# Attention in a two-layer tower: score products for the next maxima moved between the score products, value products of four tiles in one row, squares last on VectorE

## The chip, the cores and the metric

The kernel runs on one core of one Trainium2 chip. The metric is the device time of one execution in microseconds (us), median over several executions. A core has five engines with a queue each, worked in order: TensorE (PE; its weight loads stand in the profile as PEld), VectorE (DVE), ScalarE (ACT), GpSimd (POOL) and SyncE (SP, used here for transfers). Engines wait for each other through semaphores only.

## What is computed

Thirty-two sequences of 512 tokens with 64 features go through an embedding and then four blocks, each added to its input: attention 0, a routed feed-forward block, attention 1, a mixture-of-experts block. Each block works on layer-normed features. The two attention blocks are what the change touches. Cut to the core:

```python
h = h + _L0_attn_ref(_layernorm(h), L0_attn_Wq, L0_attn_Wk)
# ... routed feed-forward ...
h = h + _L1_attn_ref(_layernorm(h), Wq, bq, Wk, bk, Wv, bv, Wo, bo)
# with, for q, k (and v) projected from the normed x:
scores = jnp.einsum('bsd,btd->bst', q, k) * d ** -0.5
weights = jax.nn.softmax(scores, axis=-1)
attn = jnp.einsum('bst,btd->bsd', weights, v)
```

## The kernel before, in words

All activations stay in on-chip memory (tensor `H`). The kernel goes through the phases one after the other: embedding, attention 0 (signals `a0`), routed block (`f0`), attention 1 (`a1`), mixture (`f1`). Each phase runs over the 32 sequences, one sequence per step, as a software pipeline: every engine has its own list of instructions for step i, and some of them work for sequences i+1 to i+5. The helpers `sweep` and `sweep4` run the step's body: a few steps written out at both ends and a hardware loop over the middle (steps 4 to 25, on PE and POOL 4 to 23). The order of the work is written by hand; there is no planner.

One step i of attention before the change, engine by engine:

- PE, `body` (L1033): `spread_max(i)` (L983, four small products that turn the negated row maxima of sequence i into a row; waits until all four maxima of i are there), `project(i+1)` (L965, L969 and L970), the turns of the normed features of i+2 (L927), the score products `scores(i, 0)` and `scores(i, 1)` (L997, two products each, L1005 and L1006; the first waits for ACT's copy of the maxima row, those from tile 2 on for the exponential of the tile two before), `turn_back(i-1)` (L941, L952, the output of the sequence before), `scores(i, 2)`, `scores(i, 3)`, `scores_for_max(i+1, 0)` and `(i+1, 1)` (L972, L980), `values(i, 0)` and `(i, 1)` (L1008, L1014), `scores_for_max(i+1, 2)` and `(i+1, 3)`, `values(i, 2)` and `(i, 3)`. `scores_for_max` writes its four tiles in turn to two banks, so that tiles 2 and 3 wait until the maxima of tiles 0 and 1 have been taken.
- DVE, `body` (L750): `squares_on` for i+4 (L646: square L648, sum L650, scale L652), `sum_on` for i+5 (L644), `low_parts(i+1)` (L726, L728; waits for ACT's `QH`), `finish(i-1)` (L737: reciprocal L741, product L743, addition to `H` L745; waits for PE's `turn_back`), `maxima(i+1)` (L731, four reductions L734, each waits for its `scores_for_max`).
- ACT, `body` (L500): output copy of i-1 (L486), the maxima row (L505), `QH` of i+1 (L492), four exponentials (L512), the copy of the turned features of i+2 (L464).
- POOL, `norms` (L407 on): for sequence i+4 the mean and the centring (L364, L370; these wait for DVE's sum), for i+3 the power (L376; waits for DVE's L652) and then three passes that make the normed features, L383 (waits until the value products that still read this buffer are done), L388 and L391.

The last step (i = 31) has no next sequence: no maxima, and the four value calls already stand behind each other. In it DVE also runs `meanwhile`: in attention 0 the first expert weights, in attention 1 `first_gate` (L863), whose masks PE turns with L1143 right behind the last `turn_back`.

Of the kernel before, what the change touches and what calls it, by code (L numbers as in the profile page):

```python
# [28 lines left out]
NT = SEQ // P  # L29
# [138 lines left out]
def known(i):  # L168
    return isinstance(i, int)


def has(i):

    return not known(i) or i < NSEQ


def tower_kernel(nc, tokens, route, pack, experts, out, ids_dram, pos_dram):
# [3 lines left out]
    with ExitStack() as ctx:  # L181
# [77 lines left out]
        def f32(ap):  # L259
            return ap.bitcast(F32)  # L260
# [319 lines left out]
        def _(dve):  # L580
# [62 lines left out]
            def norm_sum(s, i, par):  # L643
                v.tensor_reduce(stat[:, par, 0, :], hb(i), axis=AX, op=ALU.add).then_inc(s.sum_ready, 1)  # L644
# [65 lines left out]
            def sum_on(s, after, i, par):  # L710

                if has(i):
                    norm_sum(s, i, par)
                elif after is not None:
                    dve.wait_ge(s.h_done, i - NSEQ + 1)
                    norm_sum(after, i - NSEQ, par)

            def squares_on(s, after, i, par):
                if has(i):
                    norm_squares(s, i, par)  # L720
                elif after is not None:
                    norm_squares(after, i - NSEQ, par)

            def attention(s, after, base, meanwhile):

                def low_parts(i, par):  # L726
                    dve.wait_ge(s.qh_ready, i + 1)
                    v.tensor_tensor(Q2[:, par, :], bank[1][:, :], f32(QH[:, par, :]),  # L728
                                    ALU.subtract).then_inc(s.ql_ready, 1)

                def maxima(i, par):  # L731
                    for t in range(NT):
                        dve.wait_ge(s.s_ps, i * NT + (t + 1))
                        v.tensor_reduce(nmax[:, par, t:t + 1], bank[2 + t % 2][:, :], axis=AX, op=ALU.max,  # L734
                                        negate=True).then_inc(s.max_ready, 1)

                def finish(i, par):  # L737
                    o = bank[7][:, 0:NT * BACK].rearrange("p (t d) -> p t d", t=NT)
                    dve.wait_ge(s.back_ps, i + 1)
                    c = base + i * 2  # L740
                    v.reciprocal(rec[:, :], o[:, :, D]).then_inc(dve_chain, 1)  # L741
                    dve.wait_ge(dve_chain, c + 1)
                    v.tensor_tensor(ON[:, :, :], o[:, :, 0:D], over(rec[:, :], D), ALU.mult).then_inc(dve_chain, 1)  # L743
                    dve.wait_ge(dve_chain, c + 2)
                    v.tensor_tensor(hb(i), hb(i), ON[:, :, :], ALU.add).then_inc(s.h_done, 1)  # L745

                low_parts(0, 0)
                maxima(0, 0)

                def body(i, par):  # L750
                    squares_on(s, after, i + 4, par)
                    sum_on(s, after, i + 5, 1 - par)
                    if has(i + 1):
                        low_parts(i + 1, 1 - par)
                    if not known(i) or i >= 1:
                        finish(i - 1, 1 - par)
                    if has(i + 1):
                        maxima(i + 1, 1 - par)

                sweep(dve, body)  # L760
                meanwhile()
                finish(NSEQ - 1, 1)
# [124 lines left out]
        def _(pe):  # L887
# [74 lines left out]
            def attention(s, before, after, layer, meanwhile, rest_before=None):  # L962


                def project(i, par):  # L965
                    pe.wait_ge(s.x2_ready, i + 1)
                    if not known(i) or i >= 1:
                        pe.wait_ge(s.ql_ready, i)
                    mm(bank[1][:, :], AH[:, layer, :], X2[:, par, :], start=True, stop=False)  # L969
                    mm(bank[1][:, :], AL[:, layer, :], X2[:, par, :], start=False, stop=True).then_inc(s.q_ps, 1)  # L970

                def scores_for_max(i, par, t):  # L972

                    if t == 0:
                        pe.wait_ge(s.qh_ready, i + 1)
                    if t >= 2:
                        pe.wait_ge(s.max_ready, i * NT + (t - 1))
                    elif not known(i) or i >= 1:
                        pe.wait_ge(s.max_ready, i * NT + (t - 1))
                    mm(bank[2 + t % 2][:, :], QH[:, par, t * P:(t + 1) * P], X2[:, par, :],  # L980
                       start=True, stop=True).then_inc(s.s_ps, 1)

                def spread_max(i, par):  # L983

                    pe.wait_ge(s.max_ready, i * NT + NT)
                    if before is not None and known(i) and i == 0:
                        pe.wait_ge(before.h_done, NSEQ)
                    if not known(i) or i >= 1:
                        pe.wait_ge(s.m_ready, i)
                    if not known(i) or i >= 2:  # L990
                        pe.wait_ge(s.h_done, i - 1)
                    for t in range(NT):
                        last = mm(bank[7][:, t * P:(t + 1) * P], nmax[:, par, t:t + 1].to_broadcast([P, P]),  # L993
                                  IR[:, :], start=True, stop=True)
                    last.then_inc(s.m_ps, 1)

                def scores(i, par, kt):  # L997

                    if kt == 0:
                        pe.wait_ge(s.m_ready, i + 1)  # L1000
                    if kt >= 2 or not known(i) or i >= 1:
                        pe.wait_ge(s.e_ready, i * NT + (kt - 1))
                    cols = slice(kt * P, (kt + 1) * P)
                    o = bank[4 + kt % 2][:, :]
                    mm(o, X2[:, par, cols], QH[:, par, :], start=True, stop=False)  # L1005
                    mm(o, X2[:, par, cols], Q2[:, par, :], start=False, stop=True).then_inc(s.st_ps, 1)  # L1006

                def values(i, par, lane, kt):  # L1008

                    pe.wait_ge(s.e_ready, i * NT + (kt + 1))  # L1010
                    if kt == 0 and (not known(i) or i >= 1):
                        pe.wait_ge(s.ot_ready, i)
                    for h in range(2):
                        last = mm(bank[6][h * D:(h + 1) * D, 0:HALF], XN[:, lane, kt, :],  # L1014
                                  PT[:, par, kt, h * HALF:(h + 1) * HALF], start=(kt == 0), stop=(kt == NT - 1))
                    if kt == NT - 1:
                        last.then_inc(s.o_ps, 1)

                if before is None:
                    turn(s, 0, 0)  # L1020
                else:
                    pe.wait_ge(before.h0_ready, NSEQ)
                    pe.wait_ge(before.h1_ready, NSEQ)
                    pe.wait_ge(before.h2_ready, NSEQ)
                project(0, 0)
                if before is None:
                    turn(s, 1, 1)
                else:
                    rest_before()
                for t in range(NT):  # L1030
                    scores_for_max(0, 0, t)

                def body(i, par, lane):  # L1033
                    spread_max(i, par)
                    if has(i + 1):
                        project(i + 1, 1 - par)
                    turn_on(s, after, i + 2, par)
                    scores(i, par, 0)
                    scores(i, par, 1)
                    if not known(i) or i >= 1:  # L1040
                        turn_back(s, before, i - 1, 1 - par)
                    scores(i, par, 2)
                    scores(i, par, 3)
                    if has(i + 1):
                        scores_for_max(i + 1, 1 - par, 0)
                        scores_for_max(i + 1, 1 - par, 1)
                    if not has(i + 1):
                        pe.wait_ge(s.ql_ready, NSEQ)
                        meanwhile()
                    values(i, par, lane, 0)  # L1050
                    values(i, par, lane, 1)
                    if has(i + 1):
                        scores_for_max(i + 1, 1 - par, 2)
                        scores_for_max(i + 1, 1 - par, 3)
                    values(i, par, lane, 2)
                    values(i, par, lane, 3)

                sweep4(pe, body)
                turn_back(s, before, NSEQ - 1, 1)

# [247 lines left out]
```

## Time and profile before

| what | value |
|---|---|
| median of 3 runs | 1017.17 us (1013.14 to 1017.37) |
| the profiled execution's own time | 1015.07 us |
| its span, first to last instruction | 1013.3 us |
| mean granted TensorE clock | 0.978 of full speed |
| busy share of the span | PE 92%, PEld 62%, DVE 65%, ACT 53%, POOL 48% |
| attention 0 lies at about | 78 to 319 us |
| attention 1 lies at about | 461 to 705 us |

How to read it: the profile is one execution. Times in rows are microseconds from the span's start unless they are marked ns. A group's row gives the line of the kernel, the engine, the operation, output and input tiles and the count. A timeline row gives start, duration, engine, line and operation; "x8" merges neighbours of one kind, and the bracket is the idle time of the engine before it with what ended that. Matmuls are pipelined: the next one starts before the one before has ended.

### The profile page before, as it was taken

Reading aid. Unit: us, or ns where it says so; the run is one execution under the profiler, and the core shown is the slowest. Engines: PE = TensorE matmul, PEld = TensorE weight load, DVE = VectorE, ACT = ScalarE, POOL = GpSimd, SP = SyncE. Lnnn points to the kernel's source line nnn. Section 1 sums busy time; section 2 is a strip of 40 time slices with the busy share of each in tenths; the row PEclk is TensorE's granted clock in tenths of the full one; section 3 lists DMA queues with packets and bytes.
Section 4 is the critical chain, followed back from the end, with each engine's and each line's share of the span. In section 5 each row is a group of like instructions: output and inputs, shape, how many; then the busy total and the mean of one; then the engine's idle time right before and its main releaser. Section 6 shows DMA issues by size and latency. Waiting matters only on the chain.

```text
span 1013.3 us, 20527 instructions
## 1 busy us (share of the span) xinstructions
PE 927.8 (92%) x5964; PEld 631.8 (62%) x5964; DVE 661.0 (65%) x1864; ACT 540.6 (53%) x1065; POOL 490.1 (48%) x779
## 2 busy tenths in 40 slices
PE   0579999999998888888999999999999999999998
PEld 0456666666666555555666666666667666666665
DVE  1686787878887888886888888886343343343431
ACT  0234555555555555553555555556555665565564
POOL 0036555454546888894454545554434434434410
PEclk9867999999999999998999999999999999999999
DMA  8930000000000221210000000000000000000000
GB/s 8 278 99 1 2 0 0 0 0 0 1 1 29 56 63 56 59 53 1 1 1 0 0 0 0 1 1 1 12 12 16 16 10 16 16 10 16 16 11 22
DMA packets 31309, 22.35 MB, mean 22 GB/s; under 512 B 14498, under 2 KB 26914, under 8 KB 31266
## 3 DMA queue, kind: packets, MB, share of 16 engines
q1 hardware_dynamic: 31266, 21.81, 9.4%
q8 instruction: 23, 0.38, 0.2%
q14 instruction: 20, 0.16, 0.1%
HBM read 17.54 MB, written 4.26 MB: 22 GB/s over the span
## 4 chain that ended last, share of the span: by engine, by line
PE 72%; DVE 11%; POOL 7%; issue 5%; DMA 4%; DVEq 0%; ACT 0%; SPq 0%; POOLq 0%
PE bank L1179 11%; PE bank L1005 7%; PE bank L1014 7%; PE bank L1159 7%; PE bank L1006 6%; DVE nmax L734 6%; PE bank L1160 6%; PE bank L980 6%; PE bank L927 5%; PE bank L993 4%; PE bank L952 3%; POOL stat L376 2%; PE bank L1169 2%; PE bank L969 2%; DMA pos<-posn 2%
## 5 line engine op out<-in xcount | busy, mean ns | idle before, releaser
L383 POOL TENSOR_TENSOR XN<-XC,stat 128x252 f32<-128x252 f32 x128 | 85.4, 667 | 215.4 <-PE bank L1014 210.4
L734 DVE TENSOR_REDUCE nmax<-bank 128x1 fp32r<-128x512 f32 x256 | 165.0, 686 | 34.6 <-PE bank L980 30.1
L376 POOL TENSOR_TENSOR stat<-stat,half 128x4 f32<-128x4 f32 x128 | 134.3, 1049 | 91.2 <-DVE stat L652 88.6
L512 ACT ACTIVATE PT<-bank 128x512 f32<-128x512 f32 x256 | 139.4, 595 | 46.4 <-PE bank L1006 46.4
L1014 PE MATMUL bank<-PT,XN 128*64 128x256 f32 x1024 | 138.3, 392 | 0.0
L561 ACT ACTIVATE PT<-bank 128x512 f32<-128x512 f32 x256 | 132.0, 605 | 11.2 <-PE bank L1160 11.2
L486 ACT ACTIVATE OT<-bank 128x256 f32<-128x256 f32 x96 | 36.8, 383 | 183.4 <-PE bank L1014 132.0
L1179 PE MATMUL bank<-PT,W 128*64 128x256 f32 x1024 | 122.8, 382 | 0.0
L464 ACT ACTIVATE X<-bank 128x512 fp32r<-128x512 f32 x128 | 76.4, 597 | 80.1 <-PE bank L927 80.1
L1005 PE MATMUL bank<-QH,X 128*128 128x512 f32 x256 | 116.5, 455 | 0.4 <-ACT Q L505 0.4
L1159 PE MATMUL bank<-X,WH 128*128 128x512 f32 x256 | 108.0, 422 | 0.8 <-ACT K L552 0.8
L391 POOL TENSOR_TENSOR XS<-XN,XS 128x252 fp32r<-128x252 f32 x128 | 94.5, 738 | 18.7 <-POOL XS L388 0.5
L1006 PE MATMUL bank<-Q,X 128*128 128x512 f32 x256 | 102.1, 399 | 0.0
L927 PE MATMUL bank<-W,XS 128*128 128x128 f32 x512 | 82.0, 283 | 21.8 <-POOL XS L391 21.1
L1160 PE MATMUL bank<-K,WL 80*128 80x512 f32 x256 | 101.4, 396 | 0.0
L1014 PEld LDWEIGHTS bank<-PT,XN 128*64 128x64 f32 x1024 | 62.2, 136 | 58.1 <-ACT PT L512 22.8
L364 POOL TENSOR_TENSOR stat<-stat,ninv 128x4 f32<-128x4 f32 x128 | 30.7, 240 | 136.6 <-DVE stat L644 136.6
L927 PEld LDWEIGHTS bank<-W,XS 128*128 128x128 f32 x512 | 60.4, 143 | 54.2 <-POOL XS L391 24.1
L1179 PEld LDWEIGHTS bank<-PT,W 128*64 128x64 f32 x1024 | 70.4, 136 | 33.9 <-ACT PT L561 0.4
L980 PE MATMUL bank<-X,QH 128*128 128x512 f32 x256 | 88.3, 426 | 1.7 <-DVE nmax L734 1.4
L370 POOL TENSOR_TENSOR XC<-H,stat 128x256 f32<-128x256 f32 x128 | 79.1, 618 | 20.0 <-POOL stat L364 16.3
L826 DVE TENSOR_REDUCE g<-bank 128x32 f32<-128x64 f32 x32 | 7.2, 224 | 116.2 <-PE bank L1136 116.2
(124 smaller groups left out, 1656.6 us busy)
## 6 DMA issues: line engine op xcount, KB each, us to landing
WR<-experts SPq DMA_DIRECT2D x64, 129.0 KB, 2.1
PT<-ids SPq DMA_DIRECT2D x16, 256.0 KB, 5.3
out<-H SPq DMA_DIRECT2D x32, 128.0 KB, 1.7
posb<-pos SPq DMA_DIRECT2D x16, 192.0 KB, 5.7
W<-pack SPq DMA_DIRECT2D x5, 263.0 KB, 6.5
W<-pack SPq DMA_DIRECT2D x1, 262.5 KB, 8.6
W<-pack SPq DMA_DIRECT2D x1, 65.0 KB, 4.6
tk<-tokens SPq DMA_DIRECT2D x1, 64.0 KB, 4.4
```

What stands on the lines that cost most here:

```text
L376: pl.tensor_tensor(stat[:, par, 3, :], stat[:, par, 2, :], half[:, :], ALU.pow).then_inc(sigma_done, 1)
L512: sc_.activation(PT[:, par, kt, :], bank[4 + kt % 2][:, :], ACT.Exp, scale=SCALE).then_inc(s.e_ready, 1)
L561: sc_.activation(G[:, e, :], bank[UP[e % 4]][:, :], ACT.Gelu).then_inc(f1.gelu_ready, 1)
L734: v.tensor_reduce(nmax[:, par, t:t + 1], bank[2 + t % 2][:, :], axis=AX, op=ALU.max, negate=True).then_inc(s.max_ready, 1)
L927: last = nc.tensor.transpose(bank[0][:, t * P:(t + 1) * P], f32(XS[:, par, t, :]), w("ident"))
L980: mm(bank[2 + t % 2][:, :], QH[:, par, t * P:(t + 1) * P], X2[:, par, :], start=True, stop=True).then_inc(s.s_ps, 1)
L1005: mm(o, X2[:, par, cols], QH[:, par, :], start=True, stop=False)
L1006: mm(o, X2[:, par, cols], Q2[:, par, :], start=False, stop=True).then_inc(s.st_ps, 1)
L1014: last = mm(bank[6][h * D:(h + 1) * D, 0:HALF], XN[:, lane, kt, :], PT[:, par, kt, h * HALF:(h + 1) * HALF], start=(kt == 0), stop=(kt == ...
L1159: mm(o, WH[:, a:a + HID], X2[:, par, :], start=True, stop=False)
L1160: mm(o, WL[0:D + 2 * NEXP1, a:a + HID], K2[0:D + 2 * NEXP1, par, :], start=False, stop=True)\
L1179: last = mm(bank[5 + par][h * D:(h + 1) * D, 0:HALF], w2[:, e, :], G[:, e, h * HALF:(h + 1) * HALF], start=False, stop=(e == NEXP1 - 1))
```

## The change

On PE the four `scores_for_max` of the next sequence move: tile 0 goes between `scores(i, 1)` and `turn_back`, tile 1 between `scores(i, 2)` and `scores(i, 3)`, tiles 2 and 3 behind `scores(i, 3)`. The four `values` calls then follow each other without anything between. On DVE the four maxima are parted: two behind `low_parts`, then `finish`, then two more; squares and sums go to the end of the step. No instruction is added or removed, and buffers and semaphores stay as they are.

```diff
@@ -728,8 +728,8 @@
-                def maxima(i, par):
-                    for t in range(NT):
+                def maxima(i, par, tiles):
+                    for t in tiles:
                         dve.wait_ge(s.s_ps, i * NT + (t + 1))
                         v.tensor_reduce(nmax[:, par, t:t + 1], bank[2 + t % 2][:, :], axis=AX, op=ALU.max,
                                         negate=True).then_inc(s.max_ready, 1)
@@ -745,17 +745,18 @@
                 low_parts(0, 0)
-                maxima(0, 0)
+                maxima(0, 0, range(NT))
 
                 def body(i, par):
-                    squares_on(s, after, i + 4, par)
-                    sum_on(s, after, i + 5, 1 - par)
                     if has(i + 1):
                         low_parts(i + 1, 1 - par)
+                        maxima(i + 1, 1 - par, range(2))
                     if not known(i) or i >= 1:
                         finish(i - 1, 1 - par)
                     if has(i + 1):
-                        maxima(i + 1, 1 - par)
+                        maxima(i + 1, 1 - par, range(2, NT))
+                    squares_on(s, after, i + 4, par)
+                    sum_on(s, after, i + 5, 1 - par)
@@ -1037,23 +1038,22 @@
                     turn_on(s, after, i + 2, par)
                     scores(i, par, 0)
                     scores(i, par, 1)
+                    if has(i + 1):
+                        scores_for_max(i + 1, 1 - par, 0)
                     if not known(i) or i >= 1:
                         turn_back(s, before, i - 1, 1 - par)
                     scores(i, par, 2)
+                    if has(i + 1):
+                        scores_for_max(i + 1, 1 - par, 1)
                     scores(i, par, 3)
                     if has(i + 1):
-                        scores_for_max(i + 1, 1 - par, 0)
-                        scores_for_max(i + 1, 1 - par, 1)
+                        scores_for_max(i + 1, 1 - par, 2)
+                        scores_for_max(i + 1, 1 - par, 3)
                     if not has(i + 1):
                         pe.wait_ge(s.ql_ready, NSEQ)
                         meanwhile()
-                    values(i, par, lane, 0)
-                    values(i, par, lane, 1)
-                    if has(i + 1):
-                        scores_for_max(i + 1, 1 - par, 2)
-                        scores_for_max(i + 1, 1 - par, 3)
-                    values(i, par, lane, 2)
-                    values(i, par, lane, 3)
+                    for kt in range(NT):
+                        values(i, par, lane, kt)
```

## Rows read from the trace of the kernel before

**Rows 1.** The page, busy time by engine over the whole span.

```profile
PE 927.8 (92%) x5964; PEld 631.8 (62%) x5964; DVE 661.0 (65%) x1864; ACT 540.6 (53%) x1065; POOL 490.1 (48%) x779
```

**Rows 2.** Line L505, one per step: attention 0, attention 1, loop of attention 0.

```profile
L505 ACT ACTIVATE Q<-bank x31: 586/587/589, 92.3 to 312.0; 1x512 fp32r<-1x512 f32 x31
...
L505 ACT ACTIVATE Q<-bank x30: 586/587/591, 477.6 to 690.0; 1x512 fp32r<-1x512 f32 x30
...
L505 ACT ACTIVATE Q<-bank x20: 586/587/589, 121.6 to 261.1; 1x512 fp32r<-1x512 f32 x20
```

**Rows 3.** Chain that ended last, end of one step: start, duration, what.

```profile
274.23 0.69 DVE nmax L734
```

**Rows 4.** Timeline of PE over one step of attention 0: start, duration, instruction.

```profile
267.70 0.66 PE L993 MATMUL bank<-IR,nmax 128*128 128x128 f32 x4
...
269.85 0.40 PE L1006 MATMUL bank<-Q,X 128*128 128x512 f32 x1
270.08 0.61 PE L952 MATMUL bank<-W,OT 128*128 128x130 f32 x4
...
270.80 0.40 PE L1006 MATMUL bank<-Q,X 128*128 128x512 f32 x1
...
271.52 0.62 PE L980 MATMUL bank<-X,QH 128*128 128x512 f32 x2
272.07 1.08 PE L1014 MATMUL bank<-PT,XN 128*64 128x256 f32 x8
273.08 0.72 PE L980 MATMUL bank<-X,QH 128*128 128x512 f32 x2
...
274.96 0.33 PE L993 MATMUL bank<-IR,nmax 128*128 128x128 f32 x1
```

**Rows 5.** Timeline of DVE over the same step.

```profile
269.54 0.69 DVE L728 TENSOR_TENSOR Q<-bank,QH 128x512 fp32r<-128x512 f32 x1 [0.19 <-ACT QH L492]
270.73 0.18 DVE L741 RECIPROCAL rec<-bank 128x4 f32<-128x4 f32 x1 [0.49 <-PE bank L952]
...
271.51 0.42 DVE L745 TENSOR_TENSOR H<-H,ON 128x256 f32 x1
...
273.62 1.29 DVE L734 TENSOR_REDUCE nmax<-bank 128x1 fp32r<-128x512 f32 x2 [0.38 <-PE bank L980]
274.82 0.41 DVE L648 TENSOR_TENSOR SQ<-XC 128x256 f32<-128x256 f32 x1
```

**Rows 6.** Timeline of ACT over the same step: the first two exponentials.

```profile
269.81 1.09 ACT L512 ACTIVATE PT<-bank 128x512 f32<-128x512 f32 x2 [0.30 <-PE bank L1006]
```

**Rows 7.** Timeline from L648 to POOL's L364 where nothing else stands between.

```profile
467.28 0.42 DVE L648 TENSOR_TENSOR SQ<-XC 128x256 f32<-128x256 f32 x1
...
468.26 0.41 DVE L644 TENSOR_REDUCE stat<-H 128x4 f32<-128x256 f32 x1
...
468.76 0.20 POOL L364 TENSOR_TENSOR stat<-stat,ninv 128x4 f32<-128x4 f32 x1 [5.84 <-DVE stat L644]
```

**Rows 8.** Timeline of POOL before the first step, where it waits for nothing.

```profile
80.77 0.20 POOL L364 TENSOR_TENSOR stat<-stat,ninv 128x4 f32<-128x4 f32 x1
...
84.03 0.72 POOL L391 TENSOR_TENSOR XS<-XN,XS 128x252 fp32r<-128x252 f32 x1
```

**Rows 9.** Timeline around the end of attention 0: L745 beside L391.

```profile
319.09 0.73 POOL L391 TENSOR_TENSOR XS<-XN,XS 128x252 fp32r<-128x252 f32 x1
...
319.53 0.57 DVE L745 TENSOR_TENSOR H<-H,ON 128x256 f32<-128x256 f32 x1
```

**Rows 10.** Timeline of POOL in the step of rows 4: the power.

```profile
270.69 1.02 POOL L376 TENSOR_TENSOR stat<-stat,half 128x4 f32<-128x4 f32 x1
```

**Rows 11.** Timeline of the last step of attention 1: values in one row, masks.

```profile
700.87 1.95 PE L1014 MATMUL bank<-PT,XN 128*64 128x256 f32 x16
...
702.59 0.17 DVE L852 TENSOR_SCALAR MK<-took 128x32 bf16<-128x32 f32 x1
...
703.85 0.39 PE L1143 MATMUL bank<-IB,MK 128*128 128x128 bf16 x4
```

## The prediction

> **What bounds the kernel now.** I read the page first: PE is busy 92% of the span, no other engine over 65% [rows 1]. A busy PE is not a PE without gaps, so I went to the attention phases, the only ones touched. One ACT instruction per step marks the period: attention 0 has 30 periods from 92.3 to 312.0, 7.32 us each; attention 1 has 29 from 477.6 to 690.0, also 7.32; the loop steps of attention 0 take 139.5/19 = 7.34 [rows 2]. So 62 periods (31 in each phase) of about 7.32 us, some 454 us, are what the change can touch.
>
> Next, one step by engine. It starts with the spread of the maxima at 267.70 and the next one starts at 274.96: 7.26 us, a step outside the loop [rows 4]. The chain that ended last goes through PE for most of the step, but its last piece is the fourth maximum on DVE, 274.23 to 274.91, and the spread follows 0.05 later [rows 3, 4]. PE had no work for the last stretch: the value row of eight that starts at 272.07 lets the next product start 1.01 later (273.08), 0.07 before its busy time is over; the second row ends in the same way at about 274.75, so PE waits some 0.2 us for DVE. A second cost is inside PE: each change between the value products and the 512-column products is dear. From 272.07 the value row, two score products and the second value row need 2.7 us, while sixteen value rows in one go are busy 1.95 [rows 4, 11].
>
> **The change part by part.** Times below count from the spread of a step (267.70 = 0).
>
> *PE.* The products up to `scores(i, 1)` stay: its last starts at 2.15, the next instruction at 2.38 [rows 4]. Tile 0 for the maxima now takes that place, and like two in a pair (0.62 busy, 0.23 apart) its result is there 0.39 later, at 2.77. `turn_back` starts at 2.61; from its start to the last product of `scores(i, 2)` are 0.72 us (270.08 to 270.80), so 3.33. Tile 1 starts at 3.56, result 3.95. `scores(i, 3)` and the step to the next product took 0.72 (270.80 to 271.52, of which 0.23 are that last product's own), so tile 2 starts at 3.56 + 0.72 = 4.28 and tile 3 could start at 4.51. Sixteen value products follow 0.32 after tile 3 (271.52 + 0.23 to 272.07) and hold PE for 1.95 - 0.07 = 1.88. Without a wait PE would need 6.71 us a step. The exponentials do not get in the way: the first two start at 2.11, end by 3.20, and the score products that wait for them now start at 2.99 and 3.79 [rows 6].
>
> *DVE.* `low_parts` starts at 1.84, when ACT's `QH` is there, and ends at 2.53 [rows 5]. Maximum 0 starts 0.04 after its product, at 2.81; maximum 1 after its own, at 3.99, for 0.69. A DVE instruction with nothing to wait for starts 0.08 before the last one ends (274.82 against 273.62 + 1.29). So `finish` starts at 4.60 and lasts 1.20, from 270.73 to the end of the addition at 271.93 [rows 5]: 5.80. Maxima 2 and 3 as a pair take 1.29 from 5.72: 7.01, and the next spread starts at 7.06.
>
> *The new wait.* Tile 3 needs maximum 1 out of its bank, which ends at 4.68: PE's in-order queue stands from 4.51 to 4.73. Behind it are the sixteen value products, so they start at 5.05 to 5.15 (the higher end if the weight load, hidden before, is now exposed for 0.1) and PE is free at 6.93 to 7.03. That is a hair before DVE. Both come out near the same time; DVE's 7.06 sets the period.
>
> *Squares and sums* move from ahead of `low_parts` to the end of the step, which is the same place in time: behind the last maximum, beside the next spread. On a free DVE they reach POOL's mean 1.48 us after they start [rows 7], so at 1.35 of the next step, before `low_parts` at 1.84. They are covered by that wait for `QH`; if it were gone they would cost up to 1.4 us. But they work for one sequence later than before. POOL's train from mean to the end of L391 takes 80.77 to 84.75, 3.98 us, if nothing holds it [rows 8], so it ends at 5.33. The PE turn that needs it comes at 1.0 of the step after, 8.1 on this count: 2.7 us of slack. No SP queue or DMA of this phase is moved.
>
> *Ends of phases.* In attention 1's last step squares and sum (1.39, [rows 7]) come between `finish` and `first_gate`. The masks were ready at 702.76 and used at 703.85 [rows 11]: 0.3 us late now. In attention 0 I find cover for the same shift (POOL waits for the last values there) and cost it nothing; without that cover it would be the 1.39 us at most.
>
> *Sum.* Loop steps take 0.08 longer than 7.26 today, and I keep half of it: 7.10 instead of 7.34, 0.24 x 40 = 9.6. Outside the loop 0.20 x 22 = 4.4. Less 0.3: 13.7 us. Against the profiled execution's own 1015.07 us (span 1013.3 and 1.8 around it) that is 1001.4. The median of the runs shown, 1017.17, is 2.1 higher, so about 1003. The unseen costs have two ends. If no DVE instruction starts early behind another engine's signal, two overlaps of 0.08 go: period 7.22, gain 6 us, 1011. If DVE proves shorter, PE's 6.93 decides: 24 us, 993. I take the early start, since it stands in the same timeline, behind the same kind of wait.
>
> **POOL beside `finish`: a row against a rule.** The addition to `H` reads two tensors of on-chip memory. Beside POOL's L391 it took 0.57 instead of 0.42: it ended at 320.10, 0.28 after POOL at 319.82 [rows 9]. Beside POOL's power, 270.69 to 271.71, it kept its 0.42 from 271.51 [rows 5, 10]. So the three passes block it, the power does not. In the new order the train's last pass ends at 5.33 and the addition starts at 5.38: just clear, and harmless up to 5.52, because 5.52 + 0.28 = 5.80 is when it ends anyway.
>
> The Trainium skill, "SBUF — State Buffer", section "SBUF: two separate sides", says that VectorE and GpSimd share one port pair as an exclusive lock: a VectorE operation with two SBUF inputs and a GpSimd operation block each other for the whole instruction. The trace agrees for L391 and differs for the power, where the rule would have the addition start at 271.71. By the rule the sum here stays as it is as long as the passes end before the addition; it speaks against the change otherwise, which is the second rival.
>
> **The rivals.**
>
> 1. *No change to speak of.* DVE's line from tile 1 to the spread is now maximum, `finish`, two maxima without a gap, 3.1 us, where before only a pair of maxima (1.3) hung on the last products. If register work for the loop's waits and the lost overlaps add 0.15 to 0.25 a step, the period is 7.21 to 7.31 and the time 1010 to 1016. For it: in the loop a step costs 0.08 more already. Against it: the same waits with their register work all stand in the loop today, and together they cost no more than that 0.08. Chance 0.17.
>
> 2. *Slower: POOL's passes hold up `finish`.* If POOL's train runs 0.4 us later than counted (its passes are slowed, or sum and mean come late), L391 lies across the addition. It decides from a train's end at 5.33 + 0.45 = 5.78 on, where the addition ends 0.26 late and the gain is gone. The worst is an addition that meets the whole of the pass: 0.73 + 0.28 instead of 0.42, 0.59 late, period 7.65, 62 x 0.33 = 20 us slower, 1037; halfway some 1024. For it: the margin is 0.05 us. Against it: a pass that late needs a delay for which no row speaks, since squares, sum and train are counted from stretches in which DVE and POOL were working as they will here [rows 7, 8]. Chance 0.11.
>
> 3. *More than forecast.* The maxima get ahead and PE alone decides, at 6.9: 1017 - 62 x 0.4 = 992 to 997. It needs DVE's line to lose 0.15 us, for which I see no source. Chance 0.10.
>
> **How the numbers follow.** The forecast has 0.62, with 999 to 1009 as its own range; the rivals 0.17, 0.11 and 0.10. The range leaves out the slower rival and about half of the third, and cuts the second half of the first: 996 to 1013. A measurement of this kernel can tell about 0.5%, 5 us, from no change, which is 0.08 us a period. Faster by more than that: the forecast, the third rival: 0.72. Within: 0.17. Slower: 0.11.
>
> **What would show it.** Right: L505 periods of 7.05 to 7.15; sixteen value products in one row of 1.95; a wait of PE for the maximum ahead of tile 3 of about 0.2; the last maximum still ending 0.05 before the spread; L391 ending before L745, and L745 at 0.42; `low_parts` still waiting for `QH`. Wrong: L745 over 0.6, `low_parts` starting after 1.9 because squares and sum ran into it, turns of PE waiting for POOL, or periods that stay at 7.3.

## The result, and the profile after

The median goes from 1016.5 us (1013.14 to 1017.37, 4 runs) to 1002.18 us (1001.87 to 1003.85, 4 runs): ratio 0.9866, 95% interval 0.9846 to 0.9887. That is 14.3 us, or 1.3%, faster; 1003 us was forecast. The profiled execution took 1001.87 us (span 1000.0). TensorE's granted clock was 1.00, the 2.4 GHz level, over nearly all of both attention phases (95 to 310 and 480 to 695 us in the kernel before, 95 to 303 and 475 to 681 in the changed one), so the gain there is not one of the clock.

The page, busy time by engine, against [rows 1]:

```profile
PE 914.0 (91%) x5964; PEld 640.0 (64%) x5964; DVE 635.4 (64%) x1864; ACT 547.3 (55%) x1065; POOL 485.6 (49%) x779
```

The same instructions, with 14 us less of busy PE time. A matmul's end is modelled and neighbours overlap, so this figure says little: by the page the group of value products is busy 13.7 us less (138.3 before, 124.6 now), the group of products for the maxima 21.1 more (88.3 and 109.4). The periods tell the gain. Line L505, all 32 of each attention (in the second fence the kernel before):

```profile
L505 ACT ACTIVATE Q<-bank x32: 586/587/590, 85.5 to 305.3; 1x512 fp32r<-1x512 f32 x32
L505 ACT ACTIVATE Q<-bank x32: 586/587/588, 462.9 to 683.2; 1x512 fp32r<-1x512 f32 x32
```

```profile
L505 ACT ACTIVATE Q<-bank x32: 586/587/589, 83.4 to 312.0; 1x512 fp32r<-1x512 f32 x32
L505 ACT ACTIVATE Q<-bank x32: 586/587/591, 468.6 to 697.3; 1x512 fp32r<-1x512 f32 x32
```

From these four rows the whole difference of the two spans can be laid out. Attention 0 takes 219.8 instead of 228.6 (-8.8), attention 1 takes 220.3 instead of 228.7 (-8.4): 0.277 us a period over 62. Between the two lie 157.6 instead of 156.6 (+1.0), behind the second 316.8 instead of 316.0 (+0.8), and ahead of the first 85.5 instead of 83.4 (+2.1). The sum is -13.3, the difference of the spans. The last item I put down to chance: the change moves nothing ahead of attention 0, and in the seven experiments below that stretch ended between 84.5 and 87.9. There is only one trace of the kernel before, so this is not shown.

One step of attention 0 outside the loop, PE, against [rows 4] (lines from about L750 to L1050 are one higher in the changed kernel):

```profile
262.56 0.66 PE L994 MATMUL bank<-IR,nmax 128*128 128x128 f32 x4
...
264.94 0.39 PE L981 MATMUL bank<-X,QH 128*128 128x512 f32 x1
265.16 0.61 PE L953 MATMUL bank<-W,OT 128*128 128x130 f32 x4
...
266.08 0.39 PE L981 MATMUL bank<-X,QH 128*128 128x512 f32 x1
...
266.76 0.99 PE L981 MATMUL bank<-X,QH 128*128 128x512 f32 x2
267.68 1.95 PE L1015 MATMUL bank<-PT,XN 128*64 128x256 f32 x16
269.57 0.33 PE L994 MATMUL bank<-IR,nmax 128*128 128x128 f32 x1
```

7.01 us from spread to spread. Tiles 0 and 1 stand at 2.38 and 3.52 of the step. The pair of tiles 2 and 3 is busy 0.99 instead of the 0.62 of an undisturbed pair [rows 4]: that is the wait for maximum 1 and the weight load behind it (last section). The value row starts at 5.12 and lasts 1.95. DVE and POOL over the same step, against [rows 5, 8]:

```profile
264.40 0.69 DVE L728 TENSOR_TENSOR Q<-bank,QH 128x512 fp32r<-128x512 f32 x1 [0.54 <-ACT QH L492]
265.36 0.69 DVE L734 TENSOR_REDUCE nmax<-bank 128x1 fp32r<-128x512 f32 x1 [0.27 <-PE bank L981]
266.50 0.69 DVE L734 TENSOR_REDUCE nmax<-bank 128x1 fp32r<-128x512 f32 x1 [0.45 <-PE bank L981]
267.11 0.17 DVE L741 RECIPROCAL rec<-bank 128x4 f32<-128x4 f32 x1
267.32 0.42 DVE L743 TENSOR_TENSOR ON<-bank,rec 128x256 f32<-128x256 f32 x1
267.89 0.43 DVE L745 TENSOR_TENSOR H<-H,ON 128x256 f32 x1
268.24 1.28 DVE L734 TENSOR_REDUCE nmax<-bank 128x1 fp32r<-128x512 f32 x2
269.43 0.41 DVE L648 TENSOR_TENSOR SQ<-XC 128x256 f32<-128x256 f32 x1
```

```profile
263.95 0.20 POOL L364 TENSOR_TENSOR stat<-stat,ninv 128x4 f32<-128x4 f32 x1 [3.02 <-DVE stat L644]
...
267.21 0.72 POOL L391 TENSOR_TENSOR XS<-XN,XS 128x252 fp32r<-128x252 f32 x1
```

From the second maximum on (266.50) DVE has no idle bracket: the gaps between its instructions are 0.15 us at most, and an instruction that does not need the result of the one above it starts 0.08 to 0.09 before that one ends. The last maximum ends at 269.52, the spread follows at 269.57. POOL's L391 ends at 267.93 and the addition starts at 267.89: they touch, without effect here.

### The profile page after: what moved, and what is told of

Its sections match the earlier page's. It is cut to its first block, busy times and chain, and to the rows that moved or that the text cites. A ratio compares the mean times of both kernels' runs of the same rounds, so it can differ in the third digit from the quotient of the medians.

```text
span 1000.0 us, 20527 instructions
## 1 busy us (share of the span) xinstructions
PE 914.0 (91%) x5964; PEld 640.0 (64%) x5964; DVE 635.4 (64%) x1864; ACT 547.3 (55%) x1065; POOL 485.6 (49%) x779
## 4 chain that ended last, share of the span: by engine, by line
PE 67%; POOL 12%; DVE 9%; issue 7%; DMA 5%; SPq 0%; POOLq 0%; ACT 0%; DVEq 0%
PE bank L1179 12%; PE bank L1015 9%; PE bank L1159 7%; PE bank L1160 6%; PE bank L981 5%; PE bank L928 5%; DVE nmax L734 4%; PE bank L1006 4%; POOL stat L376 4%; PE bank L1007 4%; PE bank L994 3%; PE bank L953 2%; POOL XN L383 2%; POOL XS L388 2%; DMA pos<-posn 2%
## 5 line engine op out<-in xcount | busy, mean ns | idle before, releaser
L734 DVE TENSOR_REDUCE nmax<-bank 128x1 fp32r<-128x512 f32 x256 | 170.1, 685 | 48.6 <-PE bank L981 48.4
L364 POOL TENSOR_TENSOR stat<-stat,ninv 128x4 f32<-128x4 f32 x128 | 30.6, 239 | 332.3 <-DVE stat L644 332.3
L512 ACT ACTIVATE PT<-bank 128x512 f32<-128x512 f32 x256 | 146.0, 596 | 61.6 <-PE bank L1007 56.5
L376 POOL TENSOR_TENSOR stat<-stat,half 128x4 f32<-128x4 f32 x128 | 134.4, 1050 | 91.1 <-DVE stat L652 88.6
L561 ACT ACTIVATE PT<-bank 128x512 f32<-128x512 f32 x256 | 132.0, 605 | 11.2 <-PE bank L1160 11.2
L1015 PE MATMUL bank<-PT,XN 128*64 128x256 f32 x1024 | 124.6, 385 | 0.0
L981 PE MATMUL bank<-X,QH 128*128 128x512 f32 x256 | 109.4, 430 | 7.6 <-DVE nmax L734 1.1
L1006 PE MATMUL bank<-QH,X 128*128 128x512 f32 x256 | 113.1, 442 | 0.4 <-ACT Q L505 0.4
L391 POOL TENSOR_TENSOR XS<-XN,XS 128x252 fp32r<-128x252 f32 x128 | 94.2, 736 | 18.7 <-POOL XS L388 0.5
L1015 PEld LDWEIGHTS bank<-PT,XN 128*64 128x64 f32 x1024 | 67.8, 136 | 43.3 <-ACT PT L512 15.3
L383 POOL TENSOR_TENSOR XN<-XC,stat 128x252 f32<-128x252 f32 x128 | 77.7, 607 | 10.8 <-POOL stat L376 1.6
```

Of the source, the lines that this page charges most:

```text
L376: pl.tensor_tensor(stat[:, par, 3, :], stat[:, par, 2, :], half[:, :], ALU.pow).then_inc(sigma_done, 1)
L512: sc_.activation(PT[:, par, kt, :], bank[4 + kt % 2][:, :], ACT.Exp, scale=SCALE).then_inc(s.e_ready, 1)
L561: sc_.activation(G[:, e, :], bank[UP[e % 4]][:, :], ACT.Gelu).then_inc(f1.gelu_ready, 1)
```

## The experiments

All were timed in three rounds against the kernel before on the same chip.

**1. Squares last, alone.** On the kernel before:

```diff
 def body(i, par):
-    squares_on(s, after, i + 4, par)
-    sum_on(s, after, i + 5, 1 - par)
...
     maxima(i + 1, 1 - par)
+    squares_on(s, after, i + 4, par)
+    sum_on(s, after, i + 5, 1 - par)
```

> The kernel before with one part of the change: squares and sums at the end of the DVE step, PE order untouched. My theory: the squares stay in the same place in time, so they give nothing; POOL's train from mean to L391 (3.98 us from 1.35 of the step) now lies across finish, whose addition should start at 3.81 and can be held until 0.28 after a pass of POOL, so the period goes from 7.35 to 7.35-7.55 and the time to 1016-1030 us (ends of the phases +1.8). Rival 'the squares are what gained' (the scale L652 drops from 0.57 to 0.17 and POOL's passes leave the spread): most of the 14 us, 1003-1007 us.

Measured: 1018.78 against 1017.1 us, ratio 1.0033 (1.0015 to 1.0050). The rival falls: the moved squares give nothing. Attention 0 takes 228.2 (85.3 to 313.5) and attention 1 228.7 (471.2 to 699.9), as before. The small loss lies at the ends of the phases: 157.7 us between the two instead of 156.6, and 316.8 behind the second instead of 316.0. In the steps POOL's passes did fall on `finish`. One step outside the loop of experiment 1, then all additions in the loop of attention 0:

```profile
272.54 0.61 POOL L383 TENSOR_TENSOR XN<-XC,stat 128x252 f32<-128x252 f32 x1
273.01 0.42 DVE L745 TENSOR_TENSOR H<-H,ON 128x256 f32 x1
273.11 0.80 POOL L388 TENSOR_TENSOR XS<-XC,stat 128x252 fp32r<-128x252 f32 x1
...
275.13 1.29 DVE L734 TENSOR_REDUCE nmax<-bank 128x1 fp32r<-128x512 f32 x2 [0.39 <-PE bank L980]
```

```profile
L745 DVE TENSOR_TENSOR H<-H,ON x19: 445/511/594, 118.8 to 251.1; 128x256 f32 x19
```

In the step shown the addition met only the last 0.14 of POOL's L383 and kept its 0.42; the next pass, L388, came behind the addition and took 0.80 where it takes 0.60 alone. In the loop every addition was held: 0.51 is the median and 0.59 the longest. The period did not grow for it, because DVE behind it still waits 0.39 for PE's next product for a maximum. So `finish` had slack here, which it loses in the new order.

**2. The row, alone.** On the kernel before, DVE as it was:

```diff
                         scores_for_max(i + 1, 1 - par, 1)
+                        scores_for_max(i + 1, 1 - par, 2)
+                        scores_for_max(i + 1, 1 - par, 3)
...
-                    values(i, par, lane, 0)
-                    values(i, par, lane, 1)
-                    if has(i + 1):
-                        scores_for_max(i + 1, 1 - par, 2)
-                        scores_for_max(i + 1, 1 - par, 3)
-                    values(i, par, lane, 2)
-                    values(i, par, lane, 3)
+                    for kt in range(NT):
+                        values(i, par, lane, kt)
```

> The kernel before with one part of the change: all four products for the next maxima ahead of the values, the sixteen value products in one row, DVE as before. My theory: tiles 2 and 3 then wait for maxima 0 and 1 (ends at 4.95 and 5.54 of a step) with nothing in between; tile 3 starts at 5.6, values at 5.93 and take 1.88: period 7.8, +0.45 to +0.5 a step over 62 steps, 1044-1048 us. Rival 'the row alone gains, through fewer changes between the two kinds of product': 0.25-0.33 a step less, 996-1002 us.

Measured: 1055.34 against 1017.1 us, ratio 1.0383 (1.0357 to 1.0409), slower by 38 us, some 8 more than expected. PE in experiment 2:

```profile
272.94 1.10 PE L980 MATMUL bank<-X,QH 128*128 128x512 f32 x2 [0.55 <-DVE nmax L734]
273.97 1.95 PE L1014 MATMUL bank<-PT,XN 128*64 128x256 f32 x16
275.84 0.66 PE L993 MATMUL bank<-IR,nmax 128*128 128x128 f32 x4
```

Tiles 2 and 3 each wait for a maximum, 0.55 us for the first and inside the 1.10 for the second; the row stands behind them. The row by itself is no gain: in the kernel before, the first two value calls were the work that covered those waits. Experiment 4 shows the other half.

**3. Squares first again.** On the changed kernel, `squares_on` and `sum_on` back to the head of the DVE step.

```diff
 def body(i, par):
+    squares_on(s, after, i + 4, par)
+    sum_on(s, after, i + 5, 1 - par)
...
     maxima(i + 1, 1 - par, range(2, NT))
-    squares_on(s, after, i + 4, par)
-    sum_on(s, after, i + 5, 1 - par)
```

> The changed kernel with squares and sums put back to the head of the DVE step. My theory: the period stays at 7.00-7.10 and low_parts still waits for QH; the ends of the two phases get back 1.0 + 0.8 us: 999-1002 us, the same or 1-2 us faster than the change. Rival 'squares last is a needed part': the period goes back to 7.2-7.3, 1010-1016 us.

Measured: 998.77 against 1017.1 us, ratio 0.9814 (0.9789 to 0.9840). That is 0.5% better than the change (0.9866, 0.9846 to 0.9887), and the two intervals just miss each other. The traces show about half of it. The attention phases last about what they last in the change, 219.6 and 219.4. What differs most is their ends. The end of attention 1 in the changed kernel, then in experiment 3:

```profile
686.23 0.42 DVE L745 TENSOR_TENSOR H<-H,ON 128x256 f32<-128x256 f32 x1
686.29 0.83 POOL L388 TENSOR_TENSOR XS<-XC,stat 128x252 fp32r<-128x252 f32 x1
686.57 0.83 DVE L648 TENSOR_TENSOR SQ<-XC 128x256 f32<-128x256 f32 x1
...
690.23 0.17 DVE L853 TENSOR_SCALAR MK<-took 128x32 bf16<-128x32 f32 x1
690.55 0.38 PE L1143 MATMUL bank<-IB,MK 128*128 128x128 bf16 x4 [0.61 <-DVE MK L853]
```

```profile
689.20 0.17 DVE L853 TENSOR_SCALAR MK<-took 128x32 bf16<-128x32 f32 x1
689.91 0.71 PE L953 MATMUL bank<-R,OT 128*128 128x130 f32 x4 [0.48 <-ACT OT L486]
690.46 0.39 PE L1143 MATMUL bank<-IB,MK 128*128 128x128 bf16 x4
```

With the squares last PE waits 0.61 for the masks; with the squares first they are ready before the last `turn_back`. So the third part of the change was a small loss, at the end of each phase: 156.9 us between the two attentions here (307.5 to 464.5), 157.6 in the change, 156.6 before; behind the second 316.0 here and before, 316.8 in the change. Experiment 1 has the same two losses by itself.

**4. Two value rows.** On the changed kernel, tiles 2 and 3 for the maxima back between the value calls; tiles 0 and 1 stay early.

```diff
-                        scores_for_max(i + 1, 1 - par, 2)
-                        scores_for_max(i + 1, 1 - par, 3)
...
-                    for kt in range(NT):
-                        values(i, par, lane, kt)
+                    values(i, par, lane, 0)
+                    values(i, par, lane, 1)
+                    if has(i + 1):
+                        scores_for_max(i + 1, 1 - par, 2)
+                        scores_for_max(i + 1, 1 - par, 3)
+                    values(i, par, lane, 2)
+                    values(i, par, lane, 3)
```

> The changed kernel with tiles 2 and 3 for the maxima put back between the two pairs of value products; tiles 0 and 1 stay early, DVE as in the change. My theory: tile 2's result comes at 5.80 of a step instead of 4.6, maxima 2 and 3 end at 7.13, period 7.18-7.25, 1010-1014 us: the row is worth about 10 us because it lets the last maxima start early. Rival 'early tiles alone carry it': 1002-1004 us as with the change.

Measured: 1011.41 against 1017.1 us, ratio 0.9943 (0.9926 to 0.9959). DVE in experiment 4:

```profile
277.74 0.43 DVE L745 TENSOR_TENSOR H<-H,ON 128x256 f32<-128x256 f32 x1
278.37 1.29 DVE L734 TENSOR_REDUCE nmax<-bank 128x1 fp32r<-128x512 f32 x2 [0.19 <-PE bank L981]
```

The addition ends at 278.17, and DVE then waits 0.19 for tile 2's product, which comes behind eight value products. By the ratios, early tiles 0 and 1 give some 6 us (0.9943), with DVE in the new order and its loss at the ends of the phases included, and the row on top of them some 8 (0.9866). The parted maxima on DVE were not tried by themselves.

**5. Tile 1 directly behind tile 0.** On the changed kernel:

```diff
                         scores_for_max(i + 1, 1 - par, 0)
+                        scores_for_max(i + 1, 1 - par, 1)
                     if not known(i) or i >= 1:
                         turn_back(s, before, i - 1, 1 - par)
                     scores(i, par, 2)
-                    if has(i + 1):
-                        scores_for_max(i + 1, 1 - par, 1)
```

> The changed kernel with one product moved: tile 1 for the maxima directly behind tile 0, ahead of turn_back. It takes PE's wait for maximum 1 away (end 4.1 of a step instead of 4.63, tile 3 wanted at 4.43). If nothing else held, PE alone would need 6.64 us a step. My theory: finish then starts at 4.02 and its addition at 4.80, under POOL's L391 (4.65 to 5.37), so that it ends 0.28 behind it, at 5.65 instead of 5.23; the last maximum ends at 6.85, period 6.90 (loop 6.95), 992-996 us. Rival 'POOL's passes do not hold DVE': 6.65-6.72, 977-982 us.

Measured: 990.2 against 1016.76 us, ratio 0.9728 (0.9696 to 0.9759), a little under the expected 992 to 996. POOL, DVE and PE in experiment 5:

```profile
276.70 0.72 POOL L391 TENSOR_TENSOR XS<-XN,XS 128x252 fp32r<-128x252 f32 x1
```

```profile
276.78 0.93 DVE L745 TENSOR_TENSOR H<-H,ON 128x256 f32<-128x256 f32 x1
277.63 1.27 DVE L734 TENSOR_REDUCE nmax<-bank 128x1 fp32r<-128x512 f32 x2
```

```profile
272.10 0.66 PE L994 MATMUL bank<-IR,nmax 128*128 128x128 f32 x4 [0.24 <-DVE nmax L734]
...
276.29 0.61 PE L981 MATMUL bank<-X,QH 128*128 128x512 f32 x2
```

The pair of tiles 2 and 3 is busy 0.61: no wait for a maximum is left in it. The price is where it was expected: the addition starts 0.08 after POOL's L391 and ends at 277.71, 0.29 after POOL's end at 277.42. The maxima behind it are late, and PE waits 0.24 for them. Not every step pays this in full: in the loop of attention 0 the additions take between 0.43 and 0.98, with a median of 0.87.

**6. `finish` cut short.** On the changed kernel:

```diff
-v.tensor_tensor(ON[:, :, :], o[:, :, 0:D], over(rec[:, :], D), ALU.mult).then_inc(dve_chain, 1)
+v.tensor_tensor(ON[:, :, 0:1], o[:, :, 0:1], over(rec[:, :], 1), ALU.mult).then_inc(dve_chain, 1)
...
-v.tensor_tensor(hb(i), hb(i), ON[:, :, :], ALU.add).then_inc(s.h_done, 1)
+v.tensor_tensor(hb(i)[:, :, 0:1], hb(i)[:, :, 0:1], ON[:, :, 0:1], ALU.add).then_inc(s.h_done, 1)
```

> The changed kernel with finish cut short: the product and the addition to H work on one of 64 columns only (the other 63 columns of both attention outputs are left out), some 0.5 us off DVE's line from maximum 1 to the last maximum. My theory: in the changed kernel two lines end a step at the same time, DVE's and PE's row of values, which starts late because tile 3 waits for maximum 1; cutting DVE's leaves PE's at 6.98-7.00, so 999-1002 us. Rival 'DVE's line alone sets the period': 6.64 a step, 977-980 us.

Measured: 997.93 against 1016.76 us, ratio 0.9804 (0.9772 to 0.9835). DVE and PE in experiment 6:

```profile
274.03 1.28 DVE L734 TENSOR_REDUCE nmax<-bank 128x1 fp32r<-128x512 f32 x2
```

```profile
273.19 0.99 PE L981 MATMUL bank<-X,QH 128*128 128x512 f32 x2
274.11 1.95 PE L1015 MATMUL bank<-PT,XN 128*64 128x256 f32 x16
275.99 0.66 PE L994 MATMUL bank<-IR,nmax 128*128 128x128 f32 x4
```

The last maximum is there at 275.31, 0.68 before the spread, and nothing comes of it: the pair still takes 0.99 and the row behind it ends the step. Attention 0 takes 218.5 (86.2 to 304.7) instead of 219.8, attention 1 218.8 (461.8 to 680.6) instead of 220.3. The first period of a phase differs from trace to trace (7.0 to 9.5 us over all nine); without it the phases are 1.1 and 0.9 shorter. So in the changed kernel two lines end a step within a few hundredths of each other, and shortening DVE's alone is worth about 1 us a phase. Another 0.5 and 0.7 us are saved behind the phases (157.1 and 316.1 instead of 157.6 and 316.8), where `finish` is shorter as well. The rest of the distance between the medians is not laid out.

**7. Both.** The edits of experiments 3 and 5 together.

> Both edits on the changed kernel: tile 1 directly behind tile 0, and squares and sums at the head of the DVE step, so that POOL's three passes run at the step's start again, away from finish. My theory: no wait of PE for a maximum is left and the addition keeps its 0.42; PE alone sets the step at 6.64-6.70, 976-980 us. Rival 'another wait takes its place' (low_parts, exponentials): 6.85 or more, 990 us and up.

Measured: 974.99 against 1016.76 us, ratio 0.9586 (0.9555 to 0.9616), a little under the expected 976 to 980. PE and DVE in experiment 7:

```profile
271.46 0.66 PE L994 MATMUL bank<-IR,nmax 128*128 128x128 f32 x4
...
276.20 1.95 PE L1015 MATMUL bank<-PT,XN 128*64 128x256 f32 x16
278.08 0.66 PE L994 MATMUL bank<-IR,nmax 128*128 128x128 f32 x4
```

```profile
276.13 0.43 DVE L745 TENSOR_TENSOR H<-H,ON 128x256 f32<-128x256 f32 x1
276.48 1.28 DVE L734 TENSOR_REDUCE nmax<-bank 128x1 fp32r<-128x512 f32 x2
```

The step is 6.62 us. The addition has its 0.43 back, the last maximum ends at 277.76, 0.32 before the spread, and the spread follows the value row at once. PE is the bound. This version beats both kernels: by 4.1% the one before, and by 2.8% the change (0.9586 against 0.9866).

## Why the prediction was right, point by point

*The period.* 7.06 was forecast outside the loop, 7.10 in it; measured are 7.01 in the step shown and, in the loop, 127.1/18 = 7.06, so 0.04 to 0.05 less than forecast:

```profile
L505 ACT ACTIVATE Q<-bank x19: 586/587/589, 122.1 to 249.2; 1x512 fp32r<-1x512 f32 x19
```

The steps of the working stand in the timeline: tile 0 at 2.38 (2.38), tile 1 at 3.52 (3.56), maximum 1 at 3.94 (3.99), values at 5.12 (5.05 to 5.15), last maximum's end at 6.96 (7.01). The 0.05 stand ahead of maximum 1; from there to the end of the last maximum it is 3.02, as forecast. The early start of DVE instructions is there too: the reciprocal at 267.11, 0.08 before maximum 1 ends. The end without it (1011) is out. One sign of the forecast did not come: L391 was to end 0.05 before the addition starts, and it ended 0.04 after, which costs nothing in the step shown.

*The wait for maximum 1.* PE's line behind it was forecast to end a hair before DVE's, and experiment 6 shows that the two are even. Experiments 5 and 7 show what it is worth once the other line is short as well.

*The row.* The prediction put its gain down to fewer changes on PE. Experiments 2 and 4 show that this gain can be had only with the early tiles: with late maxima the row costs 38 us, with early ones it brings 8. How much of the 8 is fewer changes and how much the earlier start of the last maxima, which wait for tile 2 in experiment 4, no run separates.

*Squares and sums.* In the steps their move gains nothing, as said: experiments 1 and 3. `low_parts` waits 0.54 for `QH`, so they stay covered.

*Ends of phases.* This term was mis-sized: 0.3 and 0 were forecast, 0.8 and 1.0 measured. In attention 1 I had costed the squares from a stretch without POOL [rows 7]. The last step has no maxima, so the squares come right behind `finish`: POOL's L388 had to wait for the addition L745 and took 0.83 instead of 0.60, and the square L648 had to wait for L388 and took 0.83 instead of 0.42 (rows under experiment 3). PE waited 0.6 for the masks instead of 0.3. In attention 0 the shift is not the 1.39 that the prediction called the most. The squares and the sum of the last step now stand behind its `finish`, which waits for `turn_back`. POOL there, in the kernel before and in the changed one:

```profile
317.78 0.61 POOL L383 TENSOR_TENSOR XN<-XC,stat 128x252 f32<-128x252 f32 x1 [2.48 <-PE bank L1014]
```

```profile
310.47 0.32 POOL L364 TENSOR_TENSOR stat<-stat,ninv 128x4 f32<-128x4 f32 x1 [0.47 <-DVE stat L644]
```

The mean L364 starts 5.2 us after the last L505 in the changed kernel (310.47) and 1.4 after it in the kernel before (313.43): a shift of 3.7. The cover was POOL's wait of 2.48 for the last values, and it is used up: L383 starts 7.3 after the last L505 instead of 5.8.

Two misses hide each other in the total: the periods gave 17.2 us instead of 14.0, the ends took 1.8 instead of 0.3, and the profiled execution's start was 2.1 later, which I put down to chance.

*The slower rival.* Its mechanism is real, and no more than a small part of it came: it decides from 5.78 for the end of POOL's train, which ended at 5.37. In the loop it already shows. L745 in the loop of attention 0, changed kernel:

```profile
L745 DVE TENSOR_TENSOR H<-H,ON x20: 424/427/520, 119.7 to 253.9; 128x256 f32 x20
```

Half stay at 0.43 or below, the longest is 0.52, so 0.09 late. In experiment 3, with POOL's passes elsewhere, none is over 0.43, and without their first periods the two phases take 0.8 and 0.3 us less. In experiment 5 the addition came 0.65 earlier in the step (4.68 instead of 5.33) and ran fully into L391: 0.93. The Trainium skill, "SBUF — State Buffer", section "SBUF: two separate sides", describes this as a lock that the first comer keeps for its whole instruction. Experiments 1 and 5 agree, one with each engine as the first: POOL's pass at 0.80, DVE's addition at 0.93. The blocked addition ended 0.29 after POOL's pass and not a full 0.42.

All nine traces together make this a rule for these instructions. 386 additions L745 (those of experiment 6, which are shorter, left out) and squares L648 started while one of POOL's three passes had more than 0.15 us left to run, and every one ended 0.27 to 0.29 after that pass; those that started with 0.13 or less of it left took 0.41 to 0.43, all but one that ran into the pass behind it. So an addition may start some 0.14 before the pass ends, which is why 0.04 of overlap did no harm. 159 others started under POOL's power L376, with up to 0.95 of it left, and all took 0.41 to 0.43: so the prediction's reading of the power, against the rule that it cites, holds.

## What to carry to other kernels

Where two engines hand tiles to each other through two banks, ask which work covers each hand-over: products for the next step that are needed early belong between independent products, and only then can the rest be put in one row. When the new order is in, look at which lines now end together; here an order that cost nothing to try (both early tiles side by side, squares back at the head) was worth another 28 us by the ratios, of which the halves alone gave 14 and 5. Moving work that is off the path also moves what it triggers, here three GpSimd passes that can lie across a VectorE addition, and it moves the work of the last step, which has less cover.

## What was not expected of the hardware

A wait in front of a 512-column product costs more than the wait, because it holds the load of the product's weights as well. Where nothing is waited for, the load runs under the product before: tile 1's starts at 265.85 for a product at 266.08, and the product lasts 0.39. Tile 3 in the same step of the changed kernel, weight load and product (maximum 1 ends at 267.19):

```profile
267.25 0.19 PEld L981 LDWEIGHTS bank<-X,QH 128*128 128x128 f32 x1 [0.53 <-DVE nmax L734]
267.25 0.50 PE L981 MATMUL bank<-X,QH 128*128 128x512 f32 x1
```

Both start behind the wait, and the product lasts 0.50, 0.11 longer. So the pair's 0.99 is the 0.62 of an undisturbed pair, 0.26 of waiting (tile 3 could have started at 266.99) and 0.11 of load; the prediction had counted 0.22 for the wait and up to 0.1 for the load. In experiment 2 the product of tile 3 starts together with its load too and lasts 0.50, and the row starts 0.11 later than the working had it; over 62 steps that is most of the 8 us by which the expectation was missed.
